# Twelve-slot loop of an expert stage written out slot by slot, in an attention and mixture-of-experts kernel on one core

## What is computed

```python
logits = jnp.einsum('th,eh->te', x, gate_w)
probs = jax.nn.softmax(logits, axis=-1)
topw, sel = jax.lax.top_k(probs, TOP_K)
topw = topw / jnp.sum(topw, axis=-1, keepdims=True)
combine = jnp.zeros((T, E), dtype=x.dtype).at[jnp.arange(T)[:, None], sel].add(topw)
gate_up = jnp.einsum('th,eoh->eto', x, w1)
g, u = jnp.split(gate_up, 2, axis=-1)
act = jax.nn.silu(g) * u
expert_out = jnp.einsum('eti,ehi->eth', act, w2)
out = jnp.einsum('eth,te->th', expert_out, combine)
```

## Time and profile before

| | us |
|---|---|
| median of three runs | 558.54 (558.28 to 558.55) |
| the profiled execution | 557.55 |
| its span, first to last instruction | 556.0 |
| expert stage, first slot transposed to last result computed | 353.6 to 516.9 |
| TensorE busy in the span | 444.1 (80%) |
| VectorE, ScalarE, GpSimd busy | 389.4, 315.1, 301.8 |

### The profile page before, as it was taken

How to read it: one execution, slowest core, us unless ns; L and a number is a source line. 1 busy time by engine, 2 the same in 40 slices (tenths; PEclk the granted TensorE clock), 3 DMA queues, 4 the chain that set the end, 5 groups by cost and what they waited for, 6 DMA issues and landing times.

```text
span 556.0 us, 15244 instructions
## 1 busy us (share of the span) xinstructions
PE 444.1 (80%) x4192; PEld 397.1 (71%) x4193; DVE 389.4 (70%) x1215; ACT 315.1 (57%) x934; POOL 301.8 (54%) x531
## 2 busy tenths in 40 slices
PE   1779889898989898989898860599999999999100
PEld 1658778777877787778777650499989999999100
DVE  7448888988988898889888855254545454545284
ACT  5357577767776777677767620255555555555100
POOL 6534357777777777777776646044434443444200
PEclk9779899999999999999999985599999999999655
DMA  7131442222322232213221115423434343331499
GB/s 228 53 109 42 128 125 85 75 80 63 89 70 82 62 91 71 82 60 92 65 80 61 50 40 134 134 88 114 127 109 120 102 124 106 116 110 66 164 399 343
DMA packets 49542, 60.30 MB, mean 108 GB/s; under 512 B 7615, under 2 KB 43082, under 8 KB 49482
## 3 DMA queue, kind: packets, MB, share of 16 engines
q1 hardware_dynamic: 38026, 38.00, 23.5%
q0 software_dynamic: 6528, 16.86, 8.8%
q10 hardware_dynamic: 4928, 4.72, 2.5%
HBM read 32.86 MB, written 23.27 MB: 101 GB/s over the span
## 4 chain that ended last, share of the span: by engine, by line
PE 55%; DVE 11%; issue 9%; ACT 9%; POOL 6%; DMA 5%; SPq 3%; POOLq 0%; ACTq 0%; DVEq 0%
PE bank L1109 13%; PE bank L1110 12%; PE bank L1111 12%; PE bank L1320 4%; DMA we_l<-expert_out 3%; DVE late L835 3%; POOL r_qk L415 2%; PE bank L1117 2%; PE bank L1142 2%; PE bank L1219 2%; PE bank L1339 1%; PE bank L1338 1%; ACT square L599 1%; ACT late L554 1%; SPq L382 1%
## 5 line engine op out<-in xcount | busy, mean ns | idle before, releaser
L527 POOL DMA_INDIRECT expert_out<-probs,late x72 | 69.9, 971 | 100.7 <-ACT probs L720 99.6
L457 POOL DMA_INDIRECT sorted_rows<-row,place_i x64 | 66.0, 1031 | 36.3 <-POOL row L451 25.4
L1067 DVE TENSOR_TENSOR xt_l<-bank,xt_h 128x256 fp32r<-128x256 f32 x72 | 30.6, 425 | 54.9 <-ACT xt_h L702 54.8
L564 ACT CAST qp_h<-bank 32x256 f16<-32x256 f32 x128 | 46.4, 363 | 35.7 <-PE bank L1142 33.4
L841 DVE TENSOR_TENSOR qp_l<-bank,qp_h 32x256 f16<-32x256 f32 x128 | 53.3, 416 | 6.0 <-ACT qp_h L564 2.9
L1109 PE MATMUL bank<-we_h,xt_h 128*128 x144 | 53.4, 371 | 0.1
L1074 DVE SCALAR_TENSOR_TENSOR probs<-xn,late,bank 128x176 f32<-128x176 f32 x72 | 28.6, 398 | 33.1 <-ACT xn L708 33.1
L1109 PE MATMUL bank<-we_h,at_h 128*128 x144 | 46.5, 323 | 1.1 <-issue 0.6
L1110 PE MATMUL bank<-we_l,xt_h 128*128 x144 | 47.1, 327 | 0.0
L1111 PE MATMUL bank<-we_h,xt_l 128*128 x144 | 47.0, 326 | 0.0
L708 ACT ACTIVATE xn<-bank 128x176 f32<-128x176 f32 x72 | 22.9, 317 | 38.8 <-PE bank L1111 38.8
(11 more groups left out here) (194 smaller groups left out, 1571.2 us busy)
## 6 DMA issues: line engine op xcount, KB each, us to landing
late<-sorted_rows SPq DMA_DIRECT2D x72, 129.0 KB, 2.1
we_f<-w_exp SPq DMA_DIRECT2D x32, 152.0 KB, 2.5
v_bd<-v_sb SPq DMA_DIRECT2D x128, 34.0 KB, 1.9
ctx_in<-ctx_t SPq DMA_DIRECT2D x32, 128.0 KB, 2.4
we_h<-expert_out SPq DMA_DIRECT2D x8, 512.0 KB, 6.9
we_l<-expert_out SPq DMA_DIRECT2D x8, 512.0 KB, 15.5
x<-x SPq DMA_DIRECT2D x3, 1024.0 KB, 6.0
out<-we_h ACTq DMA_DIRECT2D x8, 256.0 KB, 13.3
```

Of the source, the lines that this page charges most:

```text
L457: pool.indirect_dma_start(sorted_rows, bass.IndirectOffsetOnAxis(ap=place_i[:, t.slot // 2, k, t.par:t.par + 1], axis=0), row[:, k, t.slot ...
L527: pool.indirect_dma_start(expert_out, bass.IndirectOffsetOnAxis(ap=hs[:, r, D:D + 1].bitcast(U32), axis=0), y_sb[:, r % YRING, :], None, b ...
L564: act.copy(q_part(qp_h, t, g), q_bank(g)).then_inc(S["q_h_ready"], 1)
```

## The change

Each engine's loop over rings in the expert stage becomes straight code: `slots` calls 75 turns with constants, and SyncE's and GpSimd's loops are written out by Python's `for`. The turns, their order, their work and the second weight load at r = 0 and 1 stay.

```diff
@@ SyncE @@
-        with sp.Fori(1, NSLOT // RING) as j:
+        for j in range(1, NSLOT // RING):
             for r in range(RING):
@@ GpSimd @@
-        with pool.Fori(0, NSLOT // RING) as j:
+        for j in range(NSLOT // RING):
             for r in range(RING):
                 send_y(j, r)
@@ TensorE, VectorE, ScalarE @@
 def slots(eng, turn):
 
-    for r in range(RING):
-        turn(0, r, True)
-    with eng.Fori(1, NSLOT // RING) as j:
-        for r in range(RING):
-            turn(j, r, False)
-    for r in range(3):
-        turn(NSLOT // RING, r, True)
+    for i in range(NSLOT + 3):
+        turn(i // RING, i % RING, True)
```

## The result

| | before | after |
|---|---|---|
| median, lowest to highest | 558.54 us (558.28 to 558.95, 4 runs) | **550.40 us** (549.68 to 552.18, 4 runs) |
| ratio, with its 95% interval | | 0.9864 [0.984, 0.9889] |
| the profiled execution, its span | 557.55, 556.0 | 552.18, 550.4 |
| transposes of slot 0 to those of slot 71 | 353.56 to 510.20 | 353.41 to 504.99 |

The change made the kernel faster by 8.1 us in the medians, by 6.2 to 8.9 us if the interval is taken. Read in the same order as before, the page first: fewer instructions, TensorE busy for as long as it was, and with a larger share of the chain, 62% for 55%.

The account below looks back on a forecast made before the run. TensorE bounds the kernel's expert stage, its sequencer losing 6.65 us at five ring boundaries. With 5 x 0.1 us staying visible, 6.15 us go: 558.54 - 6.15 = 552.4 us, range 551.5 to 554.8.

Parts of the forecast that it names:

- the allowance for the spread of the runs: On the kernel's total time: 0.3 us added to the range for how far runs differ.
- The bound and the loss: Expert stage: TensorE alone sets middle turns at 2.1175 us; its sequencer loses 6.65 us at five ring boundaries.
- (a): TensorE's loop step, compare and taken branch at four ring boundaries: about 0.4 us each, removed by the change.
- (c): TensorE's run-time address and slot-number arithmetic at a ring's start: nine operations of 0.1 us, 0.9 us, removed.
- (d): Second weight-offset loads in a ring's first two turns, 0.65 us each: stay, leaving about 0.05 us visible per boundary, taken as 0.1.
- a lead of 0.45: TensorE's sequencer in straight code: its offset load's checks end about 0.45 us before the matching weight load runs.
- The other engines: ScalarE, VectorE, GpSimd and SyncE lose branches and register work too, but wait for TensorE: 0 us gained.
- Longer code: TensorE's instruction fetch after 404 us: about eight more code packets, 37 to 38 in all, at a price of 0.
- the second rival: TensorE's code fetch becomes the bound: eight fetches exposed 2.1 us each, 10.7 us more, 569.2 us; chance 0.05.
- The sum of 6.15 us: Total saving at the five ring boundaries: 6.65 us lost less 5 x 0.1 us left visible.

Follow-up runs that it names:

- pe_only: The kernel before with TensorE's turns alone written out, the other four engines keeping their loops: 552.31 us, ratio 0.9896 to before.
- others_only: The kernel before with ScalarE, VectorE, SyncE and GpSimd written out, TensorE keeping its loop: 558.08 us, ratio 0.9982 to before.
- loop24: The kernel before with TensorE, VectorE and ScalarE's rings one and two written out, then a loop of two passes over 24 turns: 555.15 us, ratio 0.9964.
- again_after: The changed kernel, unchanged, executed a second time: 551.76 us, ratio 0.988 to before.
- third_after: The changed kernel, unchanged, executed a third time: 551.13 us, ratio 0.9873 to before.
- again_before: The kernel before, unchanged, executed again: 558.07 us, ratio 0.999 to before.
- loop_no2nd: The kernel before with its loops, without the second weight-offset loads and their address operation (wrong offset for ten slots): 551.95 us, ratio 0.9891.
- out_no2nd: The changed kernel with weight offsets kept across rings, so no second loads: 550.62 us, ratio 0.9877 to before.
- out_all2nd: The changed kernel with a second weight-offset load in every turn: 567.82 us, ratio 1.0183 to before.

## Why the prediction came out as it did

The mechanism was right, and two of its terms had the wrong size: what the second loads leave visible (0.5 us in all, where 0.05 was measured) and the allowance for the spread of the runs (0.3 us, where medians of the same kernel, taken on several chips, lie up to 1.7 us apart). The second put the result outside: the low end of the range already counted nothing left at the boundaries.

**The bound and the loss: right.** TensorE sets the middle turns, and 6.65 us were lost at five boundaries to its sequencer. pe_only and others_only put all of it on TensorE's loop, and 6.60 of it came back.

**(a) the branches, 0.4 us each: right to a tenth, in part by luck.** loop24 has 0.50 to 0.56 us more for a taken branch and the loop head's operation, which the forecast had priced apart at 0.1, than for the one address operation that stands in their place inside its body. By the starts in the trace of before, step and branch hold the sequencer for 0.37 to 0.39 us. But the first boundary, with which the forecast compared the other four, isn't free of it: it has a MOVE of the same line, which holds it for 0.09 us. That leaves 0.3 us, where 0.36 to 0.41 was to be explained; what fills it up is the second load of the ring's first turn: it takes 0.43 to 0.50 us at the four boundaries with a taken branch, and 0.31 at the first (in loop24 0.46 at the taken branch). From the trace of before, the MOVE, then this load at turn 12 and at turn 36:

```profile
L1389 PEldq MOVE  x1: 33/33/33, 377.5 to 377.5; - x1
...
L1325 PEldq TENSOR_LOAD <-square x1: 309/309/309, 379.3 to 379.3; - x1
...
L1325 PEldq TENSOR_LOAD <-square x1: 484/484/484, 432.8 to 432.8; - x1
```

Why that load is longer there was not tried. The compare and branch alone, when taken, has 215 to 235 ns in the trace of before, and 243 in that of loop24. The figure of the Trainium skill (Advanced Engine Details and Errata, Control Flow Timing), about 108 ns for a compare and branch, lies between the 83 ns of one not taken and the more than 200 of one taken here. The measurements decide: on this engine a taken one costs twice that.

**(c) the arithmetic, nine operations of 0.1 us: slightly too low.** From each one's start to the start of what follows, the nine take 0.97 us at the first boundary of before, 0.11 each, and the MOVE of the loop's entry is a tenth that the forecast left out: 1.06 us in place of 0.9.

**(d) the second loads, and what they leave visible: a term that failed.** The forecast said that 0.50 us too many meet a lead of 0.45, so 0.05 stays visible, and then took 0.1 for safety. Measured: 0.00 at four boundaries and 0.05 at one, 0.05 us in all in place of 0.5. It isn't that the sequencer was faster. The transposes of after show it late, and show what takes it up. Here are weight load (PEld, TensorE's own, not that of the offset) and matmul (PE) of the slot's transposes, first a usual turn (17), then turn 14, which follows the two turns with second loads at the first boundary, then turn 38, the same place at the third:

```profile
389.45 0.25 PEld L1320 LDWEIGHTS bank<-ident,late 128*128 128x128 f32 x2
...
389.56 0.38 PE L1320 MATMUL bank<-ident,late 128*128 128x128 f32 x2
...
383.13 0.21 PEld L1320 LDWEIGHTS bank<-ident,late 128*128 128x128 f32 x2
...
383.20 0.38 PE L1320 MATMUL bank<-ident,late 128*128 128x128 f32 x2
...
434.00 0.20 PEld L1320 LDWEIGHTS bank<-ident,late 128*128 128x128 f32 x2
434.01 0.43 PE L1320 MATMUL bank<-ident,late 128*128 128x128 f32 x2
```

In a usual turn the weight load goes 0.11 us ahead of its matmul, in turn 14 only 0.07, and in turn 38 0.01. So there is a second cushion behind the sequencer's lead: the weight load may come up to 0.1 us late before the matmul does. The excess of about 0.05 us was there at the first boundary, as forecast, and this cushion took it. At the third boundary the sequencer was about 0.15 us late, of which 0.10 was taken and 0.05 is seen in the 8.52. That is one execution's: again_after and third_after have 8.47 and 8.48 there, and turns 26, 50 and 62 of after have the usual 0.10 us. The balance had one lead, 0.45, where it is 0.45 + 0.10.

With that the balance of the first boundary of before, which seemed to close at 0.95 of 1.03 us, is 0.50 - 0.55 + 1.06 = 1.01 us. loop24 fits: inside its body there is no loop head, but an address operation ahead of the ring's first load in its place, so nine operations again, which take 0.96 us, and 0.50 - 0.55 + 0.96 = 0.91; 0.85 and 0.91 were measured. Two errors, a cushion of 0.10 us left out and 0.16 us of operations too few, had nearly hidden each other in the check on before, and only the part without arithmetic came out wrong. That the check closed was luck.

**The other engines, 0: nothing clear of noise.** others_only has a ratio of 0.9982 [0.9955, 1.0009], which leaves room for 2.5 us less to 0.5 more; its boundaries sum to 48.74 us against 48.91 in again_before, which puts their share there at 0.2 us.

**Longer code, 0: right.** 37 packets for TensorE, the number foreseen, at no visible price; the second rival, which asked for 2.1 us for each of eight fetches, is out. The Trainium skill (Runtime: NRT & Kernel Launch, Instruction fetch mechanics) says that sequential code streams in mostly hidden; the trace of after agrees, with eight more packets and boundaries and middle turns at 2.12 us a turn.

**From the sum to a time: the term that put the result outside the range.** The sum of 6.15 us should have been 6.6; that makes 551.9 us from the same median, still inside the range. The rest of the way to 550.4, 1.5 us, is within the spread of such medians; no trace shows a second gain of that size. The forecast allowed 0.3 us for it, since three executions of before lay within 0.3 us of each other. They were no measure of it: later executions of before lie 6.1 us apart, those of after up to 5.0. Against 23 and 11 runs of before, after gains 6.8 and 7.1 us in the medians. The medians of before (558.54, 558.59, 558.07, 556.88, 558.22) lie 1.7 us apart, those of after (550.40, 551.76, 551.13) 1.4. A width of 1.5 us to each side, taken from them, would only just have held the result (551.9 - 1.5 = 550.4). One reason for the spread can be seen: between traces whose code up to there is the same, the expert stage begins at 351.1 us (again_before) to 355.1 (loop24), and both start values of the profiled pair were 353.4 to 353.6.

## What to carry to other kernels

Where the busiest engine has "issue" gaps at a loop's seam, make its sequencer's balance turn by turn: what it must do in a turn (here 1.72 us of 2.12), what a register load adds (0.65), and what lead it has; work on registers is free up to that and costs all of it beyond. Then either of two remedies, straight code or fewer register loads, may bring nearly the whole gain, and the other, added to it, nothing more. And take the width of the range from what repeated executions of such a kernel spread over, not from three that happen to agree.

## What the runs showed of the hardware beside this

**TensorE's weight load (PEld) runs ahead of its matmul by 0.10 to 0.11 us at the slot's transposes,** and hides a sequencer that is late by no more than that (above).

**One long turn, at the same slot in nearly every trace.** Turn 56 of after takes 3.32 us (table of stretches above). It takes 3.08 us in again_before, 3.12 in again_after, 3.21 in others_only, 3.38 in loop_no2nd, 3.22 in out_no2nd, 3.22 in third_after and 3.35 in loop24, but 2.32 in pe_only, and 2.11 in the first trace of before; in out_all2nd, with turns of 2.36 on average, it takes 2.32. So it goes neither with the loop nor with straight code. Nor is it code being fetched, as the expectation of again_after suspected: again_before and loop_no2nd have it, and no code packet arrives on any queue between 404 and 512 us in either. The timeline of after there, ScalarE, VectorE, then TensorE:

```profile
473.01 0.32 ACT L708 ACTIVATE xn<-bank 128x176 f32<-128x176 f32 x1 [1.92 <-remote]
...
473.36 0.40 DVE L1074 SCALAR_TENSOR_TENSOR probs<-xn,late,bank 128x176 f32<-128x176 f32 x1 [1.81 <-ACT xn L708]
...
473.81 0.14 PEld L1338 LDWEIGHTS bank<-ident,probs 128*128 128x128 f32 x1 [0.58 <-DVE probs L1074]
...
475.40 0.20 PEld L1320 LDWEIGHTS bank<-ident,late 128*128 128x128 f32 x2 [0.41 <-issue]
```

ScalarE's silu (line 708) comes late, VectorE's product behind it, and TensorE, which needs that product for its transposes, stands still. Who released ScalarE the profile doesn't name ("remote"). GpSimd, too, is late at this place in all of the traces, that first one of before among them: its sends there start 3.5 us or more apart where 2.1 are usual.

```profile
470.19 0.97 POOL L527 DMA_INDIRECT expert_out<-probs,late  x1 [1.22 <-ACT probs L720]
473.71 0.98 POOL L527 DMA_INDIRECT expert_out<-probs,late  x1 [2.55 <-ACT probs L720]
```

These two are of before. What holds ScalarE up was not tried and stays open; where it happens it costs 1.0 to 1.3 us (0.97 in again_before, 1.21 in after), and it is why the profiled pair differs by less than the boundaries say.
